# Linear attention with heads on partitions: a reordered stage of a decoder kernel

## The reference, cut to what matters

```python
x = _layernorm(x + _L1_attn_ref(x, ...))
# in _L1_attn_ref, all n, h: batch row and head; l: token; d, m: dimension in the head
q = sigmoid(proj(Wq, bq)); k = sigmoid(proj(Wk, bk)); v = proj(Wv, bv)
sink_incoming   = 1 / einsum('nhld,nhd->nhl', q + EPS, k.sum(2) + EPS)
source_outgoing = 1 / einsum('nhld,nhd->nhl', k + EPS, q.sum(2) + EPS)
conserved_sink   = einsum('nhld,nhd->nhl', q + EPS, (k * source_outgoing[..., None]).sum(2) + EPS)
conserved_source = einsum('nhld,nhd->nhl', k + EPS, (q * sink_incoming[..., None]).sum(2) + EPS)
sink_allocation    = sigmoid(conserved_sink)
source_competition = softmax(clip(conserved_source, -1, 1), axis=-1) * l
kv  = einsum('nhld,nhlm->nhdm', k, v * source_competition[..., None])
out = einsum('nhld,nhdm->nhlm', q * sink_incoming[..., None], kv) * sink_allocation[..., None]
return out @ Wo.T + bo
```

## Time and profile before

| | |
|---|---|
| median of 3 runs | 2173.53 us (2172.13 to 2187.19) |
| the profiled execution | 2181.74 us, its span 2180.0 us |
| mean granted TensorE clock | 0.896 of full |
| busy share of the span | TensorE 88%, VectorE 66%, ScalarE 45%, GpSimd 46% |
| linear attention | from about 927 to 1229 us of the span |

### The profile page before, as it was taken

How to read it: one execution, slowest core, us unless ns; L and a number is a source line. 1 busy time by engine, 2 the same in 40 slices (tenths; PEclk the granted TensorE clock), 3 DMA queues, 4 the chain that set the end, 5 groups by cost and what they waited for, 6 DMA issues and landing times. The chain is left out here.

```text
span 2180.0 us, 60448 instructions
## 1 busy us (share of the span) xinstructions
PE 1913.7 (88%) x21298; PEld 1446.5 (66%) x21298; DVE 1430.0 (66%) x3458; ACT 991.3 (45%) x1977; POOL 1000.9 (46%) x1042
## 2 busy tenths in 40 slices
PE   7999979997998499759999689999999999984665
PEld 4677758886888277548888456666676767652332
DVE  3777756775877444336766457777676767655998
ACT  2555534441111043323444245555555555534897
POOL 1333331221777443355553136565656565642443
PEclk8999989997999599968999689999999999985556
DMA  5311118992211399443331111110101010001111
GB/s 181 107 36 34 34 52 289 331 330 80 54 54 49 114 299 296 127 133 100 96 97 39 46 31 31 32 35 28 37 25 37 25 37 25 21 9 31 58 57 42
DMA packets 157099, 192.81 MB, mean 88 GB/s; under 512 B 27971, under 2 KB 140614, under 8 KB 157013
## 3 DMA queue, kind: packets, MB, share of 16 engines
q1 hardware_dynamic: 146741, 189.07, 27.7%
q0 software_dynamic: 10272, 2.62, 0.6%
HBM read 140.78 MB, written 77.51 MB: 100 GB/s over the span
## 5 line engine op out<-in xcount | busy, mean ns | idle before, releaser
L2964 DVE TENSOR_REDUCE xa_kq<-xa_A 100x4 f32<-100x1444 f32 x128 | 212.7, 1661 | 158.1 <-PE xa_A L2633 158.1
L2792 ACT ACTIVATE xa_prob<-xa_A 121x1600 f32<-121x1600 f32 x96 | 144.5, 1505 | 235.3 <-PE xa_A L2660 235.3
L2867 POOL TENSOR_TENSOR xa_prob<-xa_prob,xa_exp_bias 121x1600 f32<-121x1600 f32 x64 | 228.5, 3571 | 40.8 <-ACT xa_prob L2792 40.8
L1429 POOL DMA_INDIRECT slot_rows<-rt_x_again,rt_slot_u x150 | 154.7, 1031 | 67.5 <-issue 62.7
L2892 POOL TENSOR_TENSOR xa_o_rstd<-xa_o_var,xa_power 100x1 f32<-100x1 f32 x32 | 17.8, 555 | 241.4 <-DVE xa_o_var L3004 241.4
L2660 PEld LDWEIGHTS xa_A<-xa_q2T,xa_kqT 17*121 17x121 f32 x3072 | 92.3, 184 | 46.0 <-issue 29.0
L2633 PE MATMUL xa_A<-xa_kqT 16*100 16x361 f32 x1024 | 113.0, 511 | 6.8 <-ACT xa_prob L2792 6.8
L1675 POOL DMA_INDIRECT contrib<-ex_y,ex_place_u x64 | 62.2, 973 | 120.4 <-ACT ex_y L1727 107.9
L2660 PE MATMUL xa_A<-xa_q2T,xa_kqT 17*121 17x100 f32 x3072 | 108.5, 278 | 4.8 <-DVE xa_kq L2964 4.2
L2577 PE MATMUL xa_C<-xa_wk,xa_rows_T 128*121 128x256 f32 x384 | 103.8, 409 | 1.7 <-ACT xa_rows_T L2772 1.7
L2577 PE MATMUL xa_C<-xa_wv,xa_rows_T 128*121 128x256 f32 x384 | 101.3, 401 | 0.0
(11 more groups left out here) (352 smaller groups left out, 5150.8 us busy)
## 6 DMA issues: line engine op xcount, KB each, us to landing
ex_w<-in_w13T SPq DMA_DIRECT2D x64, 352.0 KB
contrib<-xs_zero SPq DMA_DIRECT2D x30, 640.0 KB
la_rows<-contrib SPq DMA_DIRECT2D x16, 1200.0 KB
xs_ctxT<-in_ctxT SPq DMA_DIRECT2D x32, 512.0 KB
xa_rows_t<-in_ctx SPq DMA_DIRECT2D x96, 121.0 KB
ex_w<-in_w2T SPq DMA_DIRECT2D x64, 176.0 KB
slot_rows<-xs_zero SPq DMA_DIRECT2D x32, 272.0 KB
ex_x_t<-slot_rows SPq DMA_DIRECT2D x64, 136.0 KB, 5.7
```

The lines of the kernel that those rows point to most:

```text
L1429: nc.gpsimd.indirect_dma_start(slot_rows, bass.IndirectOffsetOnAxis(slot_u[:, k, n:n + 1], 0), x_again[:, k, :], None, bounds_check=SLOTS ...
L2792: nc.scalar.activation(prob[:, n, :].rearrange("p (h a) -> p h a", h=HPG), A[:ROWS, :, 0:G * T], ACT.Exp, scale=EXP_SCALE).then_inc(exp_re ...
L2867: nc.gpsimd.tensor_tensor(chunk, chunk, exp_bias[:, n, :].unsqueeze(1).to_broadcast([ROWS, HEADS, T]), ALU.mult).then_inc(biased, 1)
L2964: nc.vector.tensor_reduce(kq[:T, k, NCH, 4 * j:4 * j + 4, DH:DH + 1].rearrange("p h o -> p (h o)"), A[:T, :, 0:src_len], axis=AXIS_X, op=A ...
```

## The change

- `against` has the weights as the stationary operand, 32 columns at a time, and the 100 tokens as the moving one. Keys and queries of both batch rows land in the four partition groups of one PSUM tile: heads are on partitions. One reciprocal of 128x100 replaces two of 100x32, and TensorE turns it round (`turn_inverse`), with a ScalarE copy (`inverse_out`) behind it.
- `weighted_sums` takes 32 columns of the inverse as the stationary operand and 256 feature columns as the moving one, in four partition groups; a mask keeps each head's own dimensions (`own_dims`, a new constant), two turns (`turn_sums`) and a ScalarE copy (`sums_out`) bring it to `wt2`.
- The softmax sum over the tokens is now along a row and comes with the exponential (`accum_out`); the matmul by ones goes. The shares are turned back by one turn (`turn_shares`), and `weigh_values` and `gain` read them from PSUM.
- `keys_values` makes 16 products of 32 by 32 in place of 4 of 128 by 128.
- TensorE's list isn't woven any more. The order is: denominators, projection quarter, keys-values, turn of the inverse, quarter, weighted sums, quarter, turn of the sums, quarter, conserved sums, attended product, turn of the shares, output projection, values, turns of q and k, turn of x (of the unit two ahead), turn of y. The attended product stands ahead of the output projection; the values stand ahead of the turns; the token turns go to PSUM tiles 7 and 4, the output projection to 4.
- `keep` (x + bias) moves from VectorE to the end of GpSimd's round, the small sum for the variance to GpSimd's `roots`. From round 2 on, GpSimd does the adds ahead of the roots. VectorE's token sums lie in PSUM. `finish` and the store come one round later.

```diff
-                def against(b, n, column, weights):
-                    two, j = divmod(n, 2 * KC)
-                    o = column + two * 2 * HEADS
-                    return nc.tensor.matmul(X[5][:T, o:o + 2 * HEADS], qke[:, k, j, two * T:(two + 1) * T], all_columns(weights, (j + KC) % (2 * KC), two),
-                                            start=(j == 0), stop=(j == 2 * KC - 1))
+                def against(b, column, weights, sums_of_other):
+                    k = b[1] % 2
+                    for c in range(KC):
+                        for of in (KEY, QUERY):
+                            for two in range(2):
+                                columns = group(1 - of if sums_of_other else of, two)
+                                last = nc.tensor.matmul(X[5][group(of, two), column:column + T], weights[:, c, columns],
+                                                        qke[:, k, place(of, c), two * T:(two + 1) * T], start=(c == 0), stop=(c == KC - 1))
+                    return last
+                def turn_inverse(b):
+                    pe.wait_ge(inverted, at(b, 1, 1))
+                    nc.tensor.transpose(X[5][:T, INV:INV + P], inv_h[:], ident[:]).then_inc(inv_turned, 1)
+                def keys_values(b):
...
+                    for two in range(2):
+                        for c in range(KC):
+                            for h in range(GROUPS):
+                                n, o = two * KC + c, c * P + 32 * h
+                                last = nc.tensor.matmul(X[6][32 * h:32 * h + 32, 32 * n:32 * n + 32], tok[:, k, two, D + o:D + o + 32],
+                                                        v[:, k, two, o:o + 32], start=True, stop=True)
+                def weighted_sums(b):
...
+                    for of in (KEY, QUERY):
+                        for two in range(2):
+                            last = nc.tensor.matmul(X[5][group(of, two), OWN:OWN + D], inv[:, k, group(of, two)],
+                                                    tok[:, k, two, (1 - of) * D:(2 - of) * D], start=True, stop=True)
-                def sum_exponentials(b):
-                    pe.wait_ge(ecs_ready, at(b, 1, 1))
-                    nc.tensor.matmul(X[5][:T, ESUM:ESUM + 2 * HEADS], ones[:], wide(ecs[:]), start=True, stop=True).then_inc(esummed, 1)
+                def turn_sums(b): ...
+                def turn_shares(b): ...
@@ TensorE, body: the new order
+                    if now: denominators(b)
+                    if coming: project(later(b, 1), 0)
+                    if prev: keys_values(later(b, -1))
+                    if now: turn_inverse(b)
+                    if coming: project(later(b, 1), 1)
+                    if now: weighted_sums(b)
+                    if coming: project(later(b, 1), 2)
+                    if now: turn_sums(b)
+                    if coming: project(later(b, 1), 3)
+                    if now: conserved(b)
+                    if prev: attend(later(b, -1))
+                    if now: turn_shares(b)
+                    if has(-2): project_out(later(b, -2), 0); project_out(later(b, -2), 1)
+                    if coming: values(later(b, 1)); turn_qk(later(b, 1), 0); turn_qk(later(b, 1), 1)
+                    if has(2): turn_rows(later(b, 2))
+                    if prev: turn_y(later(b, -1))
@@ ScalarE, body: the new order
+  inverse_out(b), finish(b-4), gates(b+1, 0), sums_out(b), gates(b+1, 1), allocate(b), gates_e(b+1),
+  normalise(b+2), tokens_out(b+1, 0), tokens_out(b+1, 1), rows_out(b+2), y_out(b-1)
@@ VectorE, body: the new order
+  invert(b), mask_kv(b-1), bias_values(b), second_weights(b), moments(b), clip(b), aggregate(b), compete(b),
+  weigh_values(b), gain(b), scale_out(b-1), residual(b-2), first_weights(b+1)
@@ GpSimd
+                def keep(b):
+                    k = b[1] % 2
+                    pool.wait_ge(x3_ready, at(b, 1, 1))
+                    pool.wait_ge(r_ready, at(later(b, -2), 1, 1))
+                    nc.gpsimd.tensor_tensor(x_bo[:, k], x_3[:, k], bo[:].unsqueeze(1).to_broadcast([T, 2, D]), ALU.add).then_inc(kept, 1)
                 def body(b, has):
-                    if has(2) or has(-3):
+                    if b[1] < 2 and (has(2) or has(-3)):
                         roots(b, has)
                     if has(3):
                         add_halves(later(b, 3), of)
                         add_rows(later(b, 3), of)
+                    if b[1] >= 2 and (has(2) or has(-3)):
+                        roots(b, has)
+                    if has(0):
+                        keep(b)
```

More of the change, by code:

```diff
@@ L1917, in body @@
                         rows_in(later(b, 4))
-                    if has(-3):
-                        store(later(b, -3))
+                    if has(-4):
+                        store(later(b, -4))
                 periods(sp, NU, FIRST, LAST, REACH, body, 4)
@@ L2068, in attend @@
-                def attend(b, n):
-                    k = b[1] % 2
-                    two, c = divmod(n, KC)
-                    if n == 0:
-                        pe.wait_ge(kv_ready, at(b, 1, 1))
-                        pe.wait_ge(y_ready, at(later(b, -1), 1, 1))
-                    last = nc.tensor.matmul(X[7][:T, n * P:(n + 1) * P], qk[:, k, c, two * T:(two + 1) * T], kv[:, two, c, :], start=True, stop=True)
-                    if n == 2 * KC - 1:
-                        last.then_inc(attended, 1)
@@ new lines, in turn_sums, with attend @@
+                def turn_sums(b):
+                    pe.wait_ge(own_ready, at(b, 1, 1))
+                    for c in range(KC):
+                        last = nc.tensor.transpose(X[5][:, TURNED + c * P:TURNED + (c + 1) * P], own_sums[:, c * P:(c + 1) * P], ident[:])
+                    last.then_inc(own_turned, 1)
+                def attend(b):
+                    k = b[1] % 2
+                    pe.wait_ge(kv_ready, at(b, 1, 1))
+                    pe.wait_ge(y_ready, at(later(b, -1), 1, 1))
+                    if b[1] + 1 < NU:
+                        pe.wait_ge(tok_ready, at(later(b, 1), 2, 1))
+                    for two in range(2):
+                        for c in range(KC):
+                            n = two * KC + c
+                            last = nc.tensor.matmul(X[7][:T, n * P:(n + 1) * P], qk[:, k, place(QUERY, c), two * T:(two + 1) * T], kv[:, two, c, :],
+                                                    start=True, stop=True)
+                    last.then_inc(attended, 1)
@@ L2109, in body @@
                 def body(b, has):
                     now, prev, coming = has(0), has(-1), has(1)
-                    for n in range(4):
-                        if prev and n < 3:
-                            keys_values(later(b, -1), n)
-                        if now:
-                            denominators(b, KC * n)
+                    if now:
+                        denominators(b)
+                    if coming:
+                        project(later(b, 1), 0)
                     if prev:
-                        keys_values(later(b, -1), 3)
+                        keys_values(later(b, -1))
@@ L2132, in body @@
-                    if now:
-                        sum_exponentials(b)
-                    if prev:
-                        turn_y(later(b, -1))
+                        project(later(b, 1), 1)
+                    if now:
+                        weighted_sums(b)
+                    if coming:
+                        project(later(b, 1), 2)
+                    if now:
+                        turn_sums(b)
+                    if coming:
+                        project(later(b, 1), 3)
+                    if now:
+                        conserved(b)
@@ L2136, in body @@
+                    if prev:
+                        attend(later(b, -1))
+                    if now:
+                        turn_shares(b)
+                    if has(-2):
+                        project_out(later(b, -2), 0)
+                        project_out(later(b, -2), 1)
                     if coming:
@@ L2363, in residual @@
                     dve.wait_ge(out_ready, at(later(b, -2), 1, 1))
-                    nc.vector.tensor_tensor(r[:, k], X[2][:T, :].rearrange("t (two d) -> t two d", two=2), x_bo[:, k], ALU.add).then_inc(r_ready, 1)
+                    nc.vector.tensor_tensor(r[:, k], X[4][:T, :].rearrange("t (two d) -> t two d", two=2), x_bo[:, k], ALU.add).then_inc(r_ready, 1)
                 def body(b, has):
-                    if has(-1):
-                        gain(later(b, -1))
                     if has(0):
@@ L2375, in body @@
                     if has(0):
-                        second_weights(b)
+                        clip(b)
+                    if has(2) or has(-3):
+                        aggregate(b, has)
+                    if has(0):
+                        compete(b)
+                        weigh_values(b)
+                        gain(b)
                     if has(-1):
```

355 lines of the change are left out of this document (175 added, 180 removed).

## The result

| | us |
|---|---|
| before, median of 4 runs beside it | 2174.22 |
| after, median of 4 runs (2143.05 to 2146.46) | 2143.34 |
| ratio, with its 95% interval | 0.9851 [0.9821, 0.9881] |
| profiled execution of after: time, span | 2143.36, 2141.6 |
| forecast | 2134 (2117 to 2160) |

The change is faster by 30.9 us (1.4%), where 39.5 had been forecast. The same three marks as before, for the profiled executions. The stage's start is GpSimd's first addition of 768 columns (933.82 after, 937.22 before); unit 2's and unit 15's first reciprocals are the row type of the earlier trace rows; the end is that of the last normalisation.

The account below looks back on a forecast made before the run. TensorE's instruction list was taken to bound each round. Units 2 to 15 minus 42.5 us, start +5 and end -2 made minus 39.5 from the median of 2173.53: 2134 us, range 2117 to 2160.

Parts of the forecast that it names:

- the ring: Output projection, residual, GpSimd's x + bias, ScalarE's normalisation, then turn of the rows, where TensorE waits 1.0 us.
- TensorE's list shrinks: TensorE's work per round falls by 4.3, from 15.4 to 11.1 us, with four partition groups side by side.
- The reciprocal: VectorE's 128x100 reciprocal takes 0.78 us, done at 1.45, so no wait before the inverse turn.
- The waits: TensorE waits per round: turn of the sums 0.3, turn of the shares 0.7, turn of the rows 1.0 us.
- The clock: TensorE's granted clock is 1.00 in settled rounds, despite turns and 2 us of waiting a round.
- Rivals 1 and 2: TensorE's clock falls once a round (2177 us, chance 0.06), or a second time per round (about 2215, chance 0.04).
- Rival 3: The four partition groups don't run side by side on TensorE: 16.3 us a round, 2180, chance 0.03.
- The fill: Rounds 0 and 1 lengthen as normalisation waits for GpSimd's x + bias; unit 2's reciprocal about 5 us later.
- the walk: Step-by-step layout of one round along TensorE from the start of the denominators, ending at 12.6 us.
- The drain: From unit 15's reciprocal to the last output: minus 2 us (bounds minus 5, plus 2).
- The round: A settled round takes 12.8 us (bounds 12.2 and 14.2), against a mean of 16.08 before.
- rival 4: Hand-over chains longer than assumed, queues having work in front: 13.6 to 14.5 us a round, 2145 to 2160, chance 0.18.

Follow-up runs that it names:

- experiment 4: Changed kernel with the first partition group's four flow-sum matmuls issued eight times, 32 in a row on one group: 2211.89 us, one execution.
- Experiment 2: Changed kernel with GpSimd's sum reading zeros in place of x, so the normalisation waits for no addition: 2119.25 us, ratio 0.9717.
- experiment 9: Changed kernel with output projection before attended product, x + bias before additions in rounds 0 and 1: 2122.41 us; with keys-values beside weighted sums too, 2119.22.
- experiment 7: Changed kernel with keys-values moved behind the second projection quarter, beside the weighted sums, and its mask moved accordingly: 2143.92 us, one execution.

## Why the prediction was right

The direction and the range held, and so did the mechanism: a shorter list, groups side by side, and the ring through four engines. The whole came as near as 9 us because errors of different signs met. By its own steps:

- **TensorE's list shrinks, and its groups run side by side: right.** Sixteen flow-sum matmuls take 0.55 us, about 0.2 of it the tail (their loads 0.33), where sixteen wide instructions took 1.7; experiment 4 measured 0.086 for one in series against the 0.083 set for it. Over the stage:

```profile
L2058 PE MATMUL la_X<-la_qke,la_wt 128*32 128x100 f32 x512 | 18.7, 266 | 0.5 <-ACT la_wt L2253 0.5
...
L2091 PE MATMUL la_X<-la_tok,la_inv 100*32 100x256 f32 x128 | 10.2, 391 | 0.4 <-ACT la_inv L2248 0.4
...
L2081 PE MATMUL la_X<-la_v,la_tok 100*32 100x32 f32 x512 | 7.7, 204 | 1.1 <-ACT la_yT L2267 1.1
```

  Before, the flow sums were busy 60.5 us in this grouping, the weighted sums 40.1 and keys-values 29.1. Weighted sums take 0.64 with their tail (taken 0.5), keys-values 0.46 (taken 0.5). The estimate of 0.7 for the weighted sums, worked out from the 2.38 of the Trainium skill, "TensorE: Matmul & The Clock Gate", Part 3, is nearer to the trace than my 0.5, if the tail is counted.
- **The reciprocal: right.** 0.78 worked out, 0.78 measured; no wait in front of the inverse turn.
- **The waits: right in place and size.** The turn of the shares 0.63 (taken 0.7), the turn of the rows 1.06 (taken 1.0), with the ring that was named. Experiment 2 cut the ring and the round went to 12.4. In front of the turn of the sums there is none (taken 0.3).
- **The clock: right, but without a reason for the part that paid.** It is 1.00 in settled rounds of which a tenth is waiting and a good part turns. My reading of the rule that transposes do not count as activity for the clock (the Trainium skill, "TensorE: Matmul & The Clock Gate", Part 4), a fall once a round, is not borne out: in each settled round the loads from 1060.86 to 1063.77 are turns and a wait alone, and the clock stays at 1.00. A longer stretch of turns alone is not shown here, so the rule itself is not tested. Rivals 1 and 2 are out (rival 1's own sum gives 2175; its last 2 us have no source). Rival 3 is out by experiment 4. But the sum also set 16.08 us, a mean with three falls of 3.1 us in it, against rounds without a fall and 1.5 us for a start at the low clock. That is 7.8 of the 42.5 us, and no reason stood for it. It came true (8.2 of the 32.65), and no run shows why the falls stopped.
- **The fill: +5.0 as forecast, its parts not.** Round 1 took 20.66 where the walk had 18.6. TensorE waits 7.6 us in it in front of the turn of the rows, as the walk has it, but it works at 1.2 GHz for some microseconds behind that wait and behind the one of round 0, which the walk left out: from the reciprocal to the turn of the shares it takes 1.3 us more than in a settled round, from the turn of the rows to the next reciprocal 1.0 more. Round 0 lost 2.0, for which the prediction had no figure of its own, and the start up to unit 0 gained 3.4 (3 forecast). That they add up to 5.0 is luck in part.
- **The drain**: -5.0 in place of -2. The granted clock averages 0.76 in the first 21 us of it before and 0.92 after, and experiment 9 shows 0.76 against 1.00 to cost 4.6 us in one and the same code. Most of the -5.0 is thus likely the clock and not the shorter list; the error of 3 us to the good is luck.
- **The round: mis-sized**, and this is the step that made the forecast 9 us short. "I take 12.8" measured 13.6, the lower edge of rival 4. Where the walk fell behind, from the start of the denominators (1050.09):

| starts | forecast | measured | late by |
|---|---|---|---|
| first quarter of the projection | 0.4 | 0.74 | 0.34 |
| keys-values | 1.05 | 1.61 | 0.56 |
| weighted sums | 2.25 | 2.93 | 0.68 |
| attended product | 4.9 | 5.75 | 0.85 |
| output projection | 6.45 | 7.45 | 1.00 |
| turn of the rows | 11.75 | 12.84 | 1.09 |

(The forecast's column is the end of the step ahead in its walk.) Most of it comes up before the attended product. The first 0.34 is mostly x transposed, which ScalarE delivers at 1050.71 as the last link of the ring; the walk had only y's copy late there. Behind the conserved sums, where nothing is late, the next load starts 0.48 us after the first, so that 0.26 of the 0.34 is x transposed and 0.08 the sums themselves. Then narrow loads start 0.24 us after wide ones have ended, in front of keys-values, weighted sums and conserved sums (the third is put down to ScalarE's copy, which ends at 1055.17 for a load at 1055.36), 0.72 in all, of which the missing wait of 0.3 in front of the turn of the sums gives some back. A wait in front of the conserved sums had been named as a sign of being wrong, and the third gap stands there. The prediction had rows with gaps of like length (0.20 and 0.21, though in front of wide loads) and priced none. Rival 4 had given "each queue has work in front of it" as the reason for a long round; the queue part fits x transposed, the gaps were in no case.

The sum: thirteen rounds 176.33 against 166.5 is +9.8, the drain -3.0, together 6.8 of the 9.3 us by which 2143.3 misses 2134. The other 2.5 is the level: I took off 8.2 us because the profiled execution lay above the median, and the changed kernel's profiled execution lies on its own (2143.36 and 2143.34) with only 5.7 less outside the stage.

The other signs were met but for two sizes: the reciprocals come every 13.5 to 13.7 us and not 12.2 to 13.5, and a flow sum takes 0.55 us and not 0.4.

What no run here settles: how the 0.24 us arises, why the clock's falls stopped, and how much of the x transposed would stay late if the ring were shorter by a link.

## What to carry to other kernels

When a list that was full is cut, find the loop that takes over, and ask which pieces of the list lie in it. Here the order of two independent pieces was worth 13 us and the place of one addition in the first two rounds 9 us, both without removing an instruction. Look at the granted clock of each stretch before you take a mean over rounds: 9 of the 209 us here were falls of the clock, and an end at another clock moved a stage by 4.6 us. Add the gap between wide and narrow loads to the price of each narrow group (measure it on the kernel's own rows), and put narrow groups side by side.

## What the hardware showed that was not expected

- The load of a 32-column tile starts 0.24 us after a run of 128-column loads has ended (in front of keys-values, weighted sums and conserved sums), and not at all behind another run of 32-column loads (experiment 7). In front of the denominators, behind the turn of y, it is 0.12. In front of full-width turns behind values (L2049) there was no gap in the changed kernel.
- Four column groups overlap although four neighbouring instructions in the list are all for one group: 0.57 us for sixteen against 0.55 by turns. With 32 for one group in a row the overlap is gone and each costs 0.086.
- VectorE's fp32 addition of 512 columns in SBUF, started 0.03 us after GpSimd's of 1536, showed 3.96 us and ended 0.55 after it. Started 0.17 us ahead of it, it took 0.69, and GpSimd's 3.84 in place of 3.44. GpSimd takes 1.26 to 1.27 for the same 512 columns.
- The clock fell with TensorE full as well as behind a wait. In the kernel before it went to 1.2 GHz three times (at 995, 1029 and 1095 us) with TensorE at work without a gap. In the changed kernel it did so in rounds 0 and 1, in TensorE's waits of 7.6 us. In settled rounds with waits of 1.06 us it never did.
